# First attention: exponentials without mask matmuls, masked afterwards by GpSimd selects

## The reference, as far as it matters

```
scores = scale * einsum('btd,bsd->bts', Q, K)
scores = where(s > t, -inf, scores)
p = exp(scores - max over s)
out = (p @ V) / max(sum over s of p, 1e-12)
```

## Time and profile before

| | us |
|---|---|
| median of 3 runs (1258.23 to 1267.85) | 1267.42 |
| the profiled execution | 1264.36 |
| its span, first to last instruction | 1262.5 |
| TensorE busy in the span (6027 matmuls) | 1031.8 |
| VectorE busy | 845.8 |
| ScalarE busy | 382.9 |
| GpSimd busy | 270.5 |

### The profile page before, as it was taken

How to read it: one execution, slowest core, us unless ns; L and a number is a source line. 1 busy time by engine, 2 the same in 40 slices (tenths; PEclk the granted TensorE clock), 3 DMA queues, 4 the chain that set the end, 5 groups by cost and what they waited for, 6 DMA issues and landing times.

```text
span 1262.5 us, 16374 instructions
## 1 busy us (share of the span) xinstructions
PE 1031.8 (82%) x6027; PEld 638.2 (51%) x6027; DVE 845.8 (67%) x2101; ACT 382.9 (30%) x622; POOL 270.5 (21%) x231
## 2 busy tenths in 40 slices
PE   4898988989989788899978872899999566898465
PEld 2254555543434466683333331667768344676344
DVE  5676657756565586656777547548556896688896
ACT  1154444533333233223332225312211122231121
POOL 3600000003222211001222210310210243333232
PEclk8698888989989997759998986899999896787786
DMA  8623030020000000000000000000000000000000
GB/s 237 156 102 77 2 77 2 3 87 1 1 1 0 1 1 1 1 2 0 1 1 0 1 0 3 1 1 1 1 1 1 0 1 1 2 2 2 1 9 25
DMA packets 9948, 25.35 MB, mean 20 GB/s; under 512 B 979, under 2 KB 7315, under 8 KB 9171
## 3 DMA queue, kind: packets, MB, share of 16 engines
q1 hardware_dynamic: 9568, 23.44, 6.6%
q10 hardware_dynamic: 294, 0.79, 0.3%
HBM read 16.69 MB, written 7.34 MB: 19 GB/s over the span
## 4 chain that ended last, share of the span: by engine, by line
PE 53%; DVE 32%; issue 6%; ACT 3%; POOL 3%; DMA 2%; SPq 0%; DVEq 0%; ACTq 0%; POOLq 0%
PE ps L686 5%; DVE a_MN L359 4%; PE ps L673 4%; PE ps L678 3%; PE ps L252 3%; DVE XN L117 2%; DVE q_E L1252 2%; DMA a_QS<-a_MT 2%; POOL rs L96 2%; PE ps L194 2%; PE ps L1513 2%; PE ps L214 2%; PE ps L1467 2%; PE ps L1510 2%; PE ps L2043 2%
## 5 line engine op out<-in xcount | busy, mean ns | idle before, releaser
L359 DVE TENSOR_REDUCE a_MN<-ps 128x1 f32<-128x384 f32 (+3 forms) x176 | 107.6, 638 | 64.3 <-PE ps L197 62.0
L96 POOL TENSOR_TENSOR rs<-t,mhalf 128x4 f32<-128x4 f32 x37 | 37.4, 1010 | 409.4 <-DVE t L90 409.3
L930 POOL TENSOR_TENSOR f_Y<-f_Y,f_TT 128x512 f32<-128x512 f32 x56 | 70.9, 1266 | 178.5 <-DVE f_TT L820 178.5
L465 ACT ACTIVATE a_PT<-ps 128x1024 f32<-128x1024 f32 x64 | 65.1, 1025 | 72.4 <-PE ps L218 71.3
L143 DVE TENSOR_TENSOR X<-ps,X 128x512 f32<-128x512 f32 x32 | 22.0, 688 | 96.1 <-PE ps L1523 49.4
L895 ACT ACTIVATE f_HH<-ps,pack_zero 128x512 f32<-128x512 f32 x64 | 44.0, 687 | 132.8 <-PE ps L673 132.8
L194 PE MATMUL ps<-a_KS,a_QS 72*128 72x128 bf16 (+3 forms) x256 | 70.9, 339 | 13.6 <-DVE a_MN L359 10.4
L686 PE MATMUL ps<-f_HH,pack_zero 128*128 128x512 f32 x128 | 74.0, 661 | 5.7 <-DVE f_TT L820 5.7
L811 DVE TENSOR_TENSOR f_XS<-ps,XNT 128x512 f32<-128x512 f32 x64 | 43.9, 688 | 46.8 <-PE ps L666 46.8
L673 PE MATMUL ps<-f_XS,pack_zero 128*128 128x512 f32 x128 | 68.5, 618 | 1.3 <-DVE f_XS L811 1.3
L820 DVE SCALAR_TENSOR_TENSOR f_TT<-ps,pack_zero,f_X 128x512 f32<-128x512 f32 x64 | 47.9, 748 | 32.2 <-PE ps L686 32.2
(11 more groups left out here) (306 smaller groups left out, 2364.9 us busy)
## 6 DMA issues: line engine op xcount, KB each, us to landing
scratch<-a_parts SPq DMA_DIRECT2D x16, 384.0 KB, 4.3
a_QS<-scratch SPq DMA_DIRECT2D x3, 1152.0 KB
a_KS<-scratch SPq DMA_DIRECT2D x9, 384.0 KB
pack_one<-in_one SPq DMA_DIRECT2D x1, 2679.5 KB, 9.4
pack_zero<-in_zero SPq DMA_DIRECT2D x1, 2607.5 KB, 16.2
a_QS<-scratch SPq DMA_DIRECT2D x4, 288.0 KB
a_KS<-scratch SPq DMA_DIRECT2D x12, 96.0 KB
X<-in_x SPq DMA_DIRECT2D x4, 256.0 KB, 10.0
```

What stands on the lines that cost most here:

```text
L96: pool.tensor_tensor(M.rs[:, 4 * b:4 * b + 4], M.t1[:, 4 * b:4 * b + 4], M.mhalf[:, 0:4], ALU.pow).then_inc(root.sem, root.tick(n, b))
L359: dve.tensor_reduce(M.a_MN[:, n % 2, ti, h0:h0 + k], bank(M, M.bank["a_max", n, jj], 128 * (ti + 1) * k).rearrange("p (a c) -> p a c", a=k ...
L465: act.activation(M.a_PT[:, c % 6, 0:1024], M.ps[:, a * 512:a * 512 + 1024], ACT.Exp).then_inc(made.sem, made.tick(n, hh))
L930: pool.tensor_tensor(M.f_Y[:, i, :], M.f_Y[:, i, :], M.f_TT[:, u % 3, :], ALU.add).then_inc(made.sem, made.tick(n, u))
```

## The change

Masks before the exponential go: `late` and `neg_st` are removed, 160 matmuls. The exponential is taken of unmasked scores. A new function on GpSimd, `seen`, sets the entries with key behind query to zero in `a_PT`, with six `affine_select` per group, and `values` waits for it. In rounds 6, 10 and 14 VectorE's `norm_back` moves from before reductions 6 to 9 to behind `normalize`. GpSimd's `norm_root` of the second norm moves between the selects.

```
-    def late(out):
-        return pe.matmul(out, M.identb[:, :], M.neg_st[:, :].unsqueeze(1).to_broadcast([128, out.shape[1], 128]), start=False, stop=True,
-                         skip_group_check=True)
...
         scores(b, h, 0, bank(M, a))
-        late(bank(M, a, 128).unsqueeze(1))
         scores(b, h, 1, bank(M, a + 1, 384))
-        scores(b, h, 3, bank(M, a + 1, 128, 384), False)
-        late(bank(M, a + 1).rearrange("p (a c) -> p a c", a=4)[:, 0:4:3, :]).then_inc(scored.sem, scored.tick(n, hh))
+        scores(b, h, 3, bank(M, a + 1, 128, 384)).then_inc(scored.sem, scored.tick(n, hh))
...
-        for u in range(2):
-            scores(b, h + u, 2, bank(M, 4, 256, 256 * u), u == 0)
-        late(bank(M, 4).rearrange("p (a c) -> p a c", a=2)[:, :, 0:128]).then_inc(scored.sem, scored.tick(n, "tail", half))
+        scores(b, h, 2, bank(M, 4, 256))
+        scores(b, h + 1, 2, bank(M, 4, 256, 256)).then_inc(scored.sem, scored.tick(n, "tail", half))
...
-        pe.wait_ge(S["a_exped"].sem, S["a_exped"].at(n, "tail", 1))
+        pe.wait_ge(S["a_seen"].sem, S["a_seen"].at(n, "tail", 1))
...
-        if g == 2 and b:
-            norm_back(dve, S, M, 1, b - 1, M.X, M.XN)
         if more:
             for jj in range(6, 10):
                 reduce(n + 2, jj)
         if n:
             normalize(n - 1)
+        if g == 2 and b:
+            norm_back(dve, S, M, 1, b - 1, M.X, M.XN)
         if more:
             reduce(n + 2, 10)
...
+    def seen(n, half):
+        made, c = S["a_seen"], 4 * n + 2 * half
+        for u in range(2):
+            P = M.a_PT[:, (c + u) % 6, 0:1024].rearrange("p (a t) -> p a t", a=2)[:, :, 0:128]
+            pool.wait_ge(S["a_exped"].sem, S["a_exped"].at(n, 2 * half + u))
+            pool.affine_select(P, P, [[0, 2], [1, 128]], ALU.is_ge, 0.0, base=0, channel_multiplier=-1).then_inc(made.sem, made.tick(n, 2 * half + u))
+        P = M.a_PT[:, c % 6:c % 6 + 2, 896:1152].rearrange("p h (a t) -> p h a t", a=2)
+        pool.wait_ge(S["a_exped"].sem, S["a_exped"].at(n, "tail", half))
+        pool.affine_select(P, P, [[0, 2], [0, 2], [1, 128]], ALU.is_ge, 0.0, base=0, channel_multiplier=-1).then_inc(made.sem, made.tick(n, "tail", half))
...
-    for b in range(4):
-        norm_root(pool, S, M, 1, b)
+    for n in range(16):
+        b, g = n // 4, n % 4
+        for half in range(2):
+            seen(n, half)
+            if half == 0 and g == 2 and b:
+                norm_root(pool, S, M, 1, b - 1)
+    norm_root(pool, S, M, 1, 3)
```

More of the change, by code:

```diff
@@ L210, in rows, with scores @@
         M.freed[bk] = (S["a_mt"], (n,))
-    def scores(b, h, si, out, first=True):
+    def scores(b, h, si, out):
         i = b % 2
-        pe.matmul(out, M.a_KS[0:75, i, h, 128 * si:128 * si + 128], M.a_QS[0:75, i, h, 128 * si:512], start=first, stop=False, skip_group_check=True)
-    def late(out):
-        return pe.matmul(out, M.identb[:, :], M.neg_st[:, :].unsqueeze(1).to_broadcast([128, out.shape[1], 128]), start=False, stop=True,
-                         skip_group_check=True)
+        return pe.matmul(out, M.a_KS[0:75, i, h, 128 * si:128 * si + 128], M.a_QS[0:75, i, h, 128 * si:512], start=True, stop=True)
     def exps(n, hh):
@@ L2343 @@
     "ident": [128, 128],
-    "identb": [128, 128], "neg_ts": [128, 128], "neg_st": [128, 128], "sel_e": [48, 8, 128],
+    "identb": [128, 128], "neg_ts": [128, 128], "sel_e": [48, 8, 128],
     "f_gate": [128, 8], "f_w1": [128, 8, 128], "f_w2": [128, 8, 128], "f_w3": [128, 8, 128],
@@ L2625, in constants @@
     c["neg_ts"] = bf(np.where(i[None, :] > i[:, None], -1e30, 0))
-    c["neg_st"] = bf(np.where(i[:, None] > i[None, :], -1e30, 0))
     e = np.zeros((48, 8, 128), np.float32)
```

## The result

| | us | ratio to before, 95% interval |
|---|---|---|
| before, 20 runs (1258.23 to 1272.5) | 1267.08 | |
| the changed kernel, 20 runs (1264.85 to 1282.86) | 1278.05 | 1.0085 (1.0065 to 1.0105) |
| its profiled execution (span 1272.6) | 1274.51 | |

1278 was measured where 1276 was forecast, and the growth is 0.0085 x 1267 = 10.8 us where the sum said 11.4. The terms of the sum did not all come out; two of them failed in opposite directions.

What follows compares the result with a forecast made beforehand. Steady groups were taken as bound by VectorE plus waits of 2.00 and 0.33 us for TensorE. Terms -4.8 + 3.8 + 6.0 + 4.8 + 1.6 = +11.4 us, on the profiled 1264.36, gave 1276 us; 8-in-10 range 1262 to 1293.

Steps and rivals of the forecast that it cites:

- Masks removed, 4.8 gained: Exponential pass on TensorE: taking out 160 mask matmuls gains 4.8 us in all, ends 3.5 and 7.6.
- The steady term: Steady groups at full clock: removed masks save 0.21 us in each of 12 groups, 2.5 us.
- the price of a slow half group: Half groups at 1.2 GHz: masks cost 0.85 us in groups 0, 5, 9 and 0.53 in 6, 10; half counted.
- rival R3: Selects of 2 us or more, or thinner TensorE work lowering the clock in steady groups: about +25 us, 1290; chance 0.20.
- norm_back moved, 3.8: Groups 6 and 10: norm_back behind normalize is no longer covered, costing 1.9 us twice, 3.8 us.
- Hold by the selects, 6.0: GpSimd's last select holds VectorE's split in eight groups (4.0 us) and norm_back in groups 6 and 10 (2.0).
- the two signs named for it: Steady groups growing from 11.2 to 11.4–11.6 us; the split's CAST or next operation growing from 0.17 to some 0.5.
- a sign that it is wrong: The split's operations, L368 to L374, staying at 0.17 us would show the forecast wrong.
- Clock behind norm_back, 4.8: Behind groups 6 and 10: TensorE's gaps bring 1.2 GHz, costing 2.4 us twice, 4.8 us.
- R1: Everything as forecast, but 2.4 GHz holds in groups 6 and 10: +6.6 us, 1271; chance 0.25.
- The end, 1.6: Last two value passes wait for selects: 1.2 us before the last, 0.4 before group 14's, together 1.6.
- R2: Masks were the bound and selects hold nothing: removal pays on the whole chain, -6.0 us or better, say 1258; chance 0.10.

## Why the prediction was right, and which terms were not

- *Masks removed, 4.8 gained.* The steady term was right in size (0.21 forecast, 0.28 measured a group: the wait before the eighth reduction halved, as read from its 0.33). So was the price of a slow half group: behind the two waits for transfers the values came 5.8 us after the wait before and 4.96 after, 0.85 less, and it was kept whole where the sum counted half. The net is still about nothing in the medians (1.0082 with the masks put back, 1.0085 without, uncertain by 4.6 us). The failing step is "That is 0.21 for each of 12 groups outside the stretches held by transfers", which let all of these keep their clock: with the masks gone it falls in some steady groups (8 of the 20 steps counted above; 0 to 1 in the changed kernel), 1.2 to 1.7 us a time. It was in rival R3 and not in the sum. (The low end given for this term, 3.5, should be 2.5 + 0.45 = 2.95; nothing else uses it.)
- *norm_back moved, 3.8.* Right: the gap it leaves is in the open. With the clock alike, the moved block costs 2.3 and 2.4 us a place, of which 0.48 is the hold by a select; that leaves 1.8 to 1.9, and the sum had 1.9.
- *Hold by the selects, 6.0.* Wrong in size: 0.33 and 0.48 us on norm_back in groups 6 and 10, and 0.23 on the split of one group, the first (0.41 us at 70.24, not 0.17), together 1.0. The step that failed is the select's duration: at 1.0 us the last one would have covered the split, at 0.64 it ends 0.04 us into it. So the two signs named for it did not come: steady groups went to 10.94 and not to 11.4, and L360 to L366 (L368 to L374 in the kernel before) stayed at a median of 0.17, which the prediction itself had named as a sign that it is wrong. The mechanism is shown by the doubled selects.
- *Clock behind norm_back, 4.8.* Right and shown: 2.7 us at group 10, and at group 6 3.6 less the 0.9 to 1.6 of a fall that came before. R1 fell.
- *The end, 1.6.* Too small: 0.5 us for the last step and, in the profile, 2.2 more in the last chain, at the low clock, which the term did not have. Against the run without selects it is 4.1. The medians leave it open below 5 us.

So -4.8 was about 0 (uncertain by 4.6), 6.0 was about 1, and these two errors, 4.8 and 5.0, cancel. With the terms as the profiles have them the sum is 0 + 3.8 + 1.0 + 5 + 2.7 = 12.5 us, where 10.8 was measured, uncertain by 2.5. That the total came within 2 us is partly luck. R2 is excluded by the steady groups: they went to 10.94, not to 10.4, and VectorE's wait before the seventh reduction, in which TensorE does the values, stayed at 2.00.

## What to carry to other kernels

Ask of a moved block not what it costs but what it stood beside: norm_back was free in the shadow of the value matmuls and cost 0.8% out of it, in the profiles about half of it through the clock of another engine. Taking work off TensorE where it isn't the bound showed no gain in the total here, and went with a lower clock in some groups; where it waits in a known gap, unused matmuls into a free bank that fit the gap paid 0.3% in the kernel before and 0.45% with selects and norm_back at home. The run that filled the waits for transfers too, and masked the last two groups on TensorE, is 0.9% below the kernel before. A helper on GpSimd beside VectorE's small SBUF operations is cheap as long as the two don't meet, and a few tenths of a microsecond decide that: lay the two timelines on each other with the helper's real duration.

## What the runs showed that I had not expected

An `affine_select` in place costs about as little as a copy (0.41 us for 256 elements, 0.64 for 512; copies of 128 and 512 take 0.35 and 0.62). TensorE's granted clock fell in a group whose longest gap was 0.72 us, while gaps of 0.55 in the kernel before left it up in all of its steady groups; and it did not fall in each such group. A CAST that overlaps the select's last 0.15 us loses nothing, one that overlaps its last 0.39 us takes 0.41 us instead of 0.17. In a doubled select a VectorE operation that starts just ahead of the next select runs freely, and the one behind it waits until that select is over.
